# Feed-forward: the product moved to the head of the slot, one pipeline stage fewer, counts shared with VectorE, and the attention's causal mask added on VectorE

## The reference, cut to what matters

```python
def ffn(x, W_syn, b_syn, W_out, b_out, gamma, beta):   # x: 2048 tokens x 512
    z = x @ ternary(W_syn).T + b_syn                   # 2048 x 2048
    thresh = top_k(z, 204)[:, -1:]                     # per row
    hidden = where(z >= thresh, relu(z), 0)
    out = hidden @ ternary(W_out).T + b_out            # 2048 x 512
    return layernorm(x + out, gamma, beta)
x = x + 0.5 * ffn(layernorm(x))
x = x + causal_attention(layernorm(x))                 # 2 sequences of 1024, 16 heads of 32
x = x + 0.5 * ffn(layernorm(x))
```

## Time and profile before

| | |
|---|---|
| median of 3 runs | 1291.21 us (1290.18 to 1293.3) |
| the profiled execution | 1289.8 us |
| its span in the trace | 1288.0 us |
| TensorE busy | 1110.0 us (86%) |
| VectorE busy | 916.6 us (71%) |
| ScalarE busy | 795.9 us (62%) |
| GpSimd busy | 297.3 us (23%) |
| first feed-forward, attention, second feed-forward | about 0 to 384, 384 to 927, 927 to 1288 us |

### The profile page before, as it was taken

The page is one execution under the profiler, slowest core; times in us unless marked ns, Lnnn a source line. Parts: engine busy times, 40 slices in busy tenths (PEclk is TensorE's granted clock), DMA queues, the critical chain, the costliest instruction groups (busy, mean ns, idle before and its releaser), DMA issues.

```text
span 1288.0 us, 17909 instructions
## 1 busy us (share of the span) xinstructions
PE 1110.0 (86%) x6149; PEld 510.9 (40%) x6198; DVE 916.6 (71%) x2010; ACT 795.9 (62%) x1147; POOL 297.3 (23%) x379
## 2 busy tenths in 40 slices
PE   0896999987768789999999799999799799998776
PEld 0342555543334333333344333332244355554333
DVE  5766899889963787875334887782223699999995
ACT  5399888896213536657614356567248998888521
POOL 2100122222252143100220450002100013222224
PEclk9997999998887989999999899999899899999787
DMA  9200000000010122110000311110000000000000
GB/s 370 72 1 1 1 1 2 1 1 1 1 33 21 50 58 50 47 38 2 1 21 8 78 47 46 31 34 2 1 1 1 1 9 10 17 18 18 17 18 33
DMA packets 22284, 37.44 MB, mean 29 GB/s; under 512 B 5398, under 2 KB 7833, under 8 KB 21532
## 3 DMA queue, kind: packets, MB, share of 16 engines
q1 hardware_dynamic: 21404, 34.54, 8.5%
q0 software_dynamic: 768, 1.57, 0.5%
HBM read 19.17 MB, written 4.21 MB: 18 GB/s over the span
## 4 chain that ended last, share of the span: by engine, by line
PE 62%; DVE 20%; issue 7%; ACT 5%; SPq 3%; POOL 1%; DMA 1%; another core or an unknown queue 1%; DVEq 0%; POOLq 0%; ACTq 0%
PE zP L473 13%; PE oP L506 11%; PE xP L619 5%; PE oP L619 5%; PE zP L603 4%; PE zP L544 4%; PE hP L582 3%; PE hP L493 3%; DVE mx L1312 3%; PE hP L644 2%; DVE arena L1095 2%; PE zP L644 2%; DVE arena L1135 2%; ACT arena L738 2%; DVE m L1143 2%
## 5 line engine op out<-in xcount | busy, mean ns | idle before, releaser
L738 ACT ACTIVATE arena<-arena,X 128x2048 int8<-128x2048 f32 x160 | 319.5, 2003 | 4.7 <-DVE X L1127 4.7
L793 ACT ACTIVATE arena<-zP,asc 128x512 f32<-128x512 f32 (+3 forms) x384 | 201.0, 581 | 115.5 <-PE zP L607 84.4
L506 PE MATMUL oP<-T,arena 128*128 128x512 f16 x1024 | 261.2, 402 | 3.0 <-DVE arena L1217 3.0
L473 PE MATMUL zP<-T,arena 128*128 128x512 f16 x1024 | 251.0, 390 | 6.0 <-ACT arena L709 5.1
L1312 DVE TENSOR_REDUCE mx<-hP 128x1 f32<-128x512 f32 (+3 forms) x256 | 135.8, 551 | 36.5 <-PE hP L585 25.0
L719 ACT ACTIVATE arena<-hP,sc 128x512 f16<-128x512 f32 x128 | 88.3, 690 | 106.8 <-PE hP L493 106.8
L473 PEld LDWEIGHTS zP<-T,arena 128*128 128x128 f16 x1024 | 102.3, 100 | 130.3 <-issue 14.6
L506 PEld LDWEIGHTS oP<-T,arena 128*128 128x128 f16 x1024 | 103.4, 102 | 112.1 <-issue 26.3
L709 ACT ACTIVATE arena<-zP,sc 128x512 f32<-128x512 f32 x128 | 87.3, 686 | 81.2 <-PE zP L478 54.8
L603 PE MATMUL zP<-arena 98*128 98x512 f16 (+3 forms) x384 | 110.2, 332 | 2.6 <-DMA arena<-arena 1.7
L1095 DVE SCALAR_TENSOR_TENSOR arena<-hP,sc,arena 128x512 f16<-128x512 f32 x128 | 95.6, 747 | 9.0 <-ACT arena L719 7.9
(11 more groups left out here) (177 smaller groups left out, 1581.6 us busy)
## 6 DMA issues: line engine op xcount, KB each, us to landing
arena<-arena SPq DMA_DIRECT2D x168, 64.0 KB, 2.0
arena<-in_w_synT SPq DMA_DIRECT2D x4, 1024.0 KB, 8.3
arena<-in_w_outT SPq DMA_DIRECT2D x4, 1024.0 KB, 14.7
out_dram<-x_sb SPq DMA_DIRECT2D x16, 256.0 KB, 2.0
x_sb<-in_x SPq DMA_DIRECT2D x3, 1024.0 KB, 14.0
arena<-in_w_o SPq DMA_DIRECT2D x2, 1024.0 KB, 5.0
arena<-arena POOLq DMA_DIRECT2D x24, 64.0 KB, 1.9
arena<-in_b_syn SPq DMA_DIRECT2D x1, 1024.0 KB, 12.1
```

What stands on the lines that cost most here:

```text
L473: pe.matmul(zP[:, c * CW:(c + 1) * CW], part[:, g % 2, k, :], T1[:, k, c * CW:(c + 1) * CW], start=(n == 0 and k == 0), stop=False)
L506: mm = pe.matmul(oP[:, :], part[:, k, :], T2[:, k, :], start=(c == 0 and n == 0 and k == 0), stop=False)
L738: act.activation(junk[:, counted[0] % 2, :], Z[:, g % ZR, :], ACT.Sign, bias=X[:, 2, k:k + 1], accum_out=S[:, k:k + 1]).then_inc(sm["cnt"], 1)
L793: act.activation(PT[:, m // 4 % 2, h, q0:512], colP[m % 3][:, q0:512], ACT.Exp, scale=asc[:, g, 10:11]).then_inc(sm["exp_done"], 1)
```

## The change

The number of the first count's slot becomes a constant, `S_CNT` = 1: count k of tile i now happens in slot i + 1 + k, so that count 0 runs in the slot of the tile's own `mm1`. `S_SEL`, `S_OUT` and `S_FIN` each go down by one (6, 7, 8), and each feed-forward has one slot fewer. The second product is no longer spread over two slots: TensorE's slot becomes `h_turn` c and `mm1` c for c = 0 to 3 (`x_turn` after c = 1), and then `mm2` 0 to 3 with `ok_rows` before chunk 2. ScalarE and VectorE's lists follow that order. Reading the flag and branching on it are taken apart, with `h_lo` 3 between. In slots 3, 4, 5 and 6 one or two of the counts are made on VectorE by `count_here` (`ON_DVE`). In the attention the mask matmul goes away and VectorE adds a bf16 mask tile while it takes the maximum (`tensor_tensor_reduce`, which also writes the sums to `scored`).

```diff
-S_SEL, S_OUT, S_FIN = 2 + NC, 3 + NC, 4 + NC
+S_CNT = 1
+S_SEL, S_OUT, S_FIN = S_CNT + NC, S_CNT + NC + 1, S_CNT + NC + 2
...
-        FIRST_UPD, LAST_UPD = 3, NT + S_SEL - 1
+        FIRST_UPD, LAST_UPD = S_CNT + 1, NT + S_SEL - 1
+        ON_DVE = {S_SEL - 3: (1,), S_SEL - 2: (1, 3), S_SEL - 1: (1, 3), S_SEL: (3,)}
...
                     for c in range(4):
+                        do(h_turn, f, s, S_OUT, c)
                         do(mm1, f, s, 1, c)
+                        if c == 1 and (f, s) != (0, 0):
+                            do(x_turn, f, s, 0)
+                    for c in range(4):
                         if c == 2:
                             do(ok_rows, f, s, S_SEL)
-                        do(h_turn, f, s, S_OUT, c)
-                        if c == 0 and (f, s) != (0, 0):
-                            do(x_turn, f, s, 0)
-                        if c < 2:
-                            do(mm2, f, s, S_OUT + 1, c + 2)
-                        else:
-                            do(mm2, f, s, S_OUT, c - 2)
+                        do(mm2, f, s, S_OUT, c)
...
-                    do(evac, f, s, 2, 3)
-                    do(h_hi, f, s, S_OUT + 1, 3)
+                    do(h_hi, f, s, S_OUT, 0)
                     do(evac, f, s, 1, 0)
-                    do(h_hi, f, s, S_OUT, 0)
+                    count(f, s, 4)
+                    do(h_hi, f, s, S_OUT, 1)
+                    do(evac, f, s, 1, 1)
                     if (f, s) != (0, 0):
                         do(x_hi, f, s, 0)
-                    count(f, s, 4)
                     count(f, s, 3)
-                    do(evac, f, s, 1, 1)
-                    do(h_hi, f, s, S_OUT, 1)
+                    do(h_hi, f, s, S_OUT, 2)
+                    do(evac, f, s, 1, 2)
+                    do(h_hi, f, s, S_OUT, 3)
+                    do(evac, f, s, 1, 3)
                     count(f, s, 2)
                     count(f, s, 1)
-                    do(evac, f, s, 1, 2)
-                    do(h_hi, f, s, S_OUT, 2)
                     count(f, s, 0)
...
+            def count_here(f, s, k):
+                i = at(s, S_CNT + k)
+                if i is None or not on_dve(s, k):
+                    return
+                g = f * NT + i
+                dve.wait_ge(sm["z_evac"], 4 * g + 4)
+                after(0)
+                link(dve.tensor_scalar(hT_mem.bitcast(I8)[:, 0:N], Z[:, g % ZR, :], X[:, 0, k:k + 1], None, ALU.is_gt, ALU.add,
+                                       accum_out=S[:, k:k + 1]))
+                link(dve.tensor_scalar(S[:, k:k + 1], S[:, k:k + 1], 2.0, -float(N), ALU.mult, ALU.add))
...
-                    do(h_lo, f, s, S_OUT + 1, 3)
+                    if s in ON_DVE and s < S_SEL:
+                        for k in range(NC):
+                            count_here(f, s, k)
+                    do(h_lo, f, s, S_OUT, 0)
+                    do(residual, f, s, S_FIN)
                     do(below, f, s, S_SEL)
-                    do(h_lo, f, s, S_OUT, 0)
+                    do(h_lo, f, s, S_OUT, 1)
                     if (f, s) != (0, 0):
                         do(x_lo, f, s, 0)
                     if (f, s) == (0, 1):
                         search_start()
                     do(pick, f, s, S_SEL)
-                    do(h_lo, f, s, S_OUT, 1)
-                    do(residual, f, s, S_FIN)
+                    if s in ON_DVE and s >= S_SEL:
+                        for k in range(NC):
+                            count_here(f, s, k)
+                    do(h_lo, f, s, S_OUT, 2)
                     if (f, s) != (0, -1):
                         do(stats1, f, s, -1)
+                    do(read_flag, f, s, S_SEL)
+                    do(h_lo, f, s, S_OUT, 3)
+                    do(search_if_open, f, s, S_SEL)
                     do(keep_top, f, s, S_SEL)
-                    do(h_lo, f, s, S_OUT, 2)
...
-                        own = c == t // 4
-                        mm = pe.matmul(rowP[bank][:, 0:w], stack[0:3 * HD, 0, h, t * P:(t + 1) * P],
-                                       stack[0:3 * HD, 1, h, 512 * c:512 * c + w], start=True, stop=not own)
-                        if own:
-                            mm = pe.matmul(rowP[bank][:, w - P:w], identm[:, :], maskq[:, :], start=False, stop=True)
...
+                        if c == t // 4:
+                            if m >= 2:
+                                dve.wait_ge(sm["row_max"], m - 1)
+                            dve.tensor_tensor_reduce(scored[:, m % 2, 0:w], rowP[bank][:, 0:w], causal[:, 512 - w:512],
+                                                     1.0, -BIG, ALU.add, ALU.max, mx[:, h, t, c:c + 1])\
+                                .then_inc(sm["row_max"], 1)
```

More of the change, by code:

```diff
@@ L220, in program @@
         identm = sb("identm", [P, P], F16)
-        maskq = sb("maskq", [P, P], F16)
+        causal = sb("causal", [P, 512], BF16)
+        scored = sb("scored", [P, 2, 512], BF16)
         maskk = sb("maskk", [P, P], F16)
@@ L361, in do, with on_dve @@
                 stage(f, i, *a)
-        FIRST_UPD, LAST_UPD = 3, NT + S_SEL - 1
+        FIRST_UPD, LAST_UPD = S_CNT + 1, NT + S_SEL - 1
+        ON_DVE = {S_SEL - 3: (1,), S_SEL - 2: (1, 3), S_SEL - 1: (1, 3), S_SEL: (3,)}
+        def on_dve(s, k):
+            return k in ON_DVE.get(s, ())
         def updates(f, s):
@@ L580, in core @@
                         w = min(512, (t + 1) * P - 512 * c)
-                        own = c == t // 4
-                        mm = pe.matmul(rowP[bank][:, 0:w], stack[0:3 * HD, 0, h, t * P:(t + 1) * P],
-                                       stack[0:3 * HD, 1, h, 512 * c:512 * c + w], start=True, stop=not own)
-                        if own:
-                            mm = pe.matmul(rowP[bank][:, w - P:w], identm[:, :], maskq[:, :], start=False, stop=True)
-                        mm.then_inc(sm["row_ps"], 1)
+                        pe.matmul(rowP[bank][:, 0:w], stack[0:3 * HD, 0, h, t * P:(t + 1) * P],
+                                  stack[0:3 * HD, 1, h, 512 * c:512 * c + w], start=True, stop=True)\
+                            .then_inc(sm["row_ps"], 1)
                     elif kind == "turn":
@@ L724, in count @@
             def count(f, s, k):
-                i = at(s, 2 + k)
-                if i is None:
+                i = at(s, S_CNT + k)
+                if i is None or on_dve(s, k):
                     return
@@ L843, in counts_before, with here @@
         def counts_before(f, s):
-            per_f = NC * NT
-            return f * per_f + sum(1 for t in range(-1, s) for k in range(NC) if at(t, 2 + k) is not None)
+            def here(upto):
+                return sum(1 for t in range(-1, upto) for k in range(NC)
+                           if at(t, S_CNT + k) is not None and not on_dve(t, k))
+            return f * here(NT + S_FIN + 1) + here(s)
         @block.gpsimd
@@ L868, in _ @@
             link(pool.tensor_scalar(identm[:, :], identf[:, :], MASK, None, ALU.mult))
-            link(pool.memset(maskq[:, :], 0.0))
+            link(pool.memset(causal[:, :], 0.0))
             link(pool.memset(maskk[:, :], 0.0))
-            pool.affine_select(out=maskq[:, :], in_=maskq[:, :], compare_op=ALU.is_ge, fill=-MASK, base=0,
-                               pattern=[[-1, P]], channel_multiplier=1).then_inc(sm["masks"], 1)
+            pool.affine_select(out=causal[:, 384:512], in_=causal[:, 384:512], compare_op=ALU.is_ge, fill=-MASK * MASK,
+                               base=0, pattern=[[-1, P]], channel_multiplier=1).then_inc(sm["masks"], 1)
             pool.affine_select(out=maskk[:, :], in_=maskk[:, :], compare_op=ALU.is_ge, fill=-MASK, base=0,
@@ L1201, in search_down, with read_flag @@
                     add_found(HIT, BOUND)
-            def keep_top(f, i):
+            def read_flag(f, i):
                 g = f * NT + i
@@ L1206, in keep_top, with search_if_open @@
                 dve.tensor_copy(oki[:, :], xP[:, 0:1]).then_inc(sm["ok_read"], 1)
+            def search_if_open(f, i):
+                g = f * NT + i
                 dve.wait_ge(sm["ok_read"], g + 1)
@@ L1209, in keep_top @@
                     search_down(Z[:, g % ZR, :])
+            def keep_top(f, i):
+                g = f * NT + i
                 dve.scalar_tensor_tensor(Z[:, g % ZR, :], Z[:, g % ZR, :], TH, Z[:, g % ZR, :], ALU.is_ge, ALU.mult)\
@@ L1248, in normal_rows @@
                     if b == 0:
-                        dve.wait_ge(sm["cnt"], NC * NT)
+                        dve.wait_ge(sm["cnt"], counts_before(1, -1))
                         dve.wait_ge(sm["x_new"], BT)
@@ L1311, in core @@
                         dve.wait_ge(sm["row_ps"], m + 1)
-                        dve.tensor_reduce(mx[:, h, t, c:c + 1], rowP[bank][:, 0:w], AX.X, ALU.max)\
-                            .then_inc(sm["row_max"], 1)
+                        if c == t // 4:
[4 more added lines that the diff above has]
+                                .then_inc(sm["row_max"], 1)
```

(4 more changed lines are left out.)

## The result

The changed kernel takes 1307.1 us (median of 4 runs, 1305.3 to 1308.6), the kernel before in the same comparison 1291.7 us (1290.2 to 1293.3). The ratio is 1.0118, 95% interval 1.0099 to 1.0137: slower by 15.4 us; the prediction said 1306. The profiled execution has a span of 1306.2 us, 18.2 more than before; it is the longest of the four, and the one before was 1.4 us under its median, so the traces show some 3 us more than the medians do.

A forecast was written before the change was run, and what follows sets the result against it. TensorE bounds full slots and the attention's row steps, VectorE the emptying. f=0 +14.4, f=1 +7.8 and attention -7 give +15.2: 1289.8 becomes 1305.0, on the median's scale 1306, range 1296 to 1317 us.

The forecast's parts named there:

- Emptying: Last slots of each block, without mm1: 17.8 us against 15.91 in f=1, 17.5 against 15.6 in f=0.
- the clock stays up: Rival for the emptying: TensorE's chunks and transposes run at full rate, 15.4 us a slot, total 1282; chance 0.11.
- Full slot: Slots with mm1 and mm2: 17.75 us in f=1, 17.45 in f=0, against TensorE's 17.24 before.
- `h_lo` 3 hides wholly behind the branch: Between flag read and keep_top on VectorE: h_lo 3 adds no time; if not hidden, up to 0.66 us more.
- First slot: Slot after the first selection, TensorE idle then restarting slow: 19.8 us in f=1, 19.5 in f=0.
- Filling: Slots up to the first keep_top: VectorE sets f=0, 115.6 against 114.2; f=1 wins 10.2 us; a count costs 2.55.
- K(6): Start of keep_top in slot 6, the first tile's selection: 115.6 us in f=0, 1003.9 in f=1.
- The end: Last tile of each block: all transposes precede mm2, product ends about 15.0 us after keep_top's start, not 17.6: -2.6 us.
- Attention: Row steps: 256 mask matmuls go, 14 us at most; VectorE's maximum costs +0.13 us each; -7 us in all.
- The order costs nothing: Rival: full slots stay at 17.24 us, emptying at 15.6 and 15.9; total 1273, down to 1266; chance 0.25.
- VectorE becomes the attention's bound: Rival for the row steps: maximum +0.33 us and more each, about +25 us per sequence, total 1355; chance 0.05.
- Gains and losses cancel: Rival: count costs its low end (-6 us in f=0), half the slots' losses come, 1288 to 1295; chance 0.12.

The follow-up runs named there:

- Experiment 3: Changed kernel plus 14 unread 512-column matmuls on TensorE ahead of the fourth transpose in each slot of the emptying: 1286.8 us, ratio 0.9971.
- experiment 1: Changed kernel with the flag's row behind the first chunk of mm2 instead of behind the second: 1297.0 us, ratio 1.0044.
- experiment 4: Attention's part alone on the kernel before: 1284.3 us; changed kernel with all counts on ScalarE: 1308.1; that with the stages back one slot: 1327.9.
- experiments 2 and 5: Changed kernel with flag's row ahead of all mm2: 1350.9 us; with h_lo 1 ahead of below: 1299.7, and that with VectorE counts only in f=1: 1302.1.

## Why the prediction was right

*How much of it is luck.* The medians moved by 15.4 us and the prediction said 15.2, but single stretches of the walk above missed by up to 3.4 us, in both directions, and cancel; against the traces the forecast is 3 us short. The kinds of slot cancel too. In f=0 the seven full slots took 123.5 us (122.2 predicted), the two behind them 35.3 (33.8) and the five of the emptying 84.4 (87.5); in f=1 it was 122.5 (124.3), 34.7 (34.4) and 86.8 (89.0). What was right is the mechanism and the sign; the last microseconds were luck.

*Emptying.* The step that decided between forecast and rivals, and shown: in f=1 17.8 us predicted, 17.8 falling to 17.1 measured, against 15.9; in f=0 17.5 predicted and only 16.6 to 17.0 measured, against 15.6. Its cause was the chain of wait, low clock, and flag's row behind two chunks. That the first slot of f=1 fits to 0.03 us is chance: two chunks took 5.71 us to the flag's row where I had 5.27, transpose and flag's row 1.23 where I had 1.36, and the branch 1.03 where I had 1.31. Experiment 3 takes the low clock alone away and gets 15.2 (the rival "the clock stays up" priced it at 15.4 and the total at 1282; made to happen, it gave 1286.8). The slot shrank from 17.8 to 17.1 us because the clock came back earlier within the two chunks: 4.6 us behind their start in the first slot and 3.1 us in the last, so that they took 5.87 us falling to 5.16 (4.62 to 5.08 in f=0). Why it comes back sooner in f=0 the runs don't show. The Trainium skill (TensorE: Matmul & The Clock Gate, What's actually happening) has the clock high only after sustained work; the granted 0.60 behind the wait and 1.00 with the added matmuls agree.

*Full slot.* 17.75 predicted, 17.55 measured in f=1: the 0.3 us for `h_lo` 1 and the flag's place were right (experiment 1: 17.22 when the row moves up). The branch was too dear in f=1, where I carried over its long level (1.31) and it came at the short one (1.03), and too cheap in the later slots of f=0, where I had the short one (1.00) and it took 1.34: those slots took 17.9 where I had 17.45. What switches the level I didn't find. The step "`h_lo` 3 hides wholly behind the branch" held, to 0.03 us.

*First slot.* 19.8 and 19.5 predicted, 20.07 and 19.16 measured.

*Filling.* K(6) in f=0 115.6 predicted, 117.2 measured; the count's 2.55 us was right to 0.03, at the upper bound. The Trainium skill (SBUF — State Buffer, Who interferes with whom) excepts a `tensor_scalar` that also writes out its accumulator from those that can enter the two-port modes; the 2.35 us of this instruction, against 1.28 for a comparison without a sum, agree, though the two also differ in the type of their output (int8 and f16). Kernels with the same filling show 115.3 to 119.0 there, so 1.6 us isn't an error that can be told. In f=1 -10.2 was predicted and -8.4 came; the sign given for it, K(6) near 1004, had left out what f=0 and the attention shift it (it came at 1016.5). What was wrong was my later reading of the parts, in the expectations of experiment 4: I held the stage for worth little and the order for the smaller cost, where they are -19.8 and +43.6. The prediction summed both in one, which is why its total held.

*The end.* -2.6 us twice was predicted, -0.9 and -1.3 came. The last tile's four chunks, TensorE in f=1:

```profile
1288.23 8.43 PE L514 MATMUL oP<-T,arena 128*128 128x512 f16 x32
```

They also start behind a wait, and 8.43 us is 1.2 more than twice the 3.62 of two chunks at the high clock. I had counted the slow return in the slots and forgotten it here.

*Attention.* -7 predicted; -6.3 in the trace, and -7.2 by the medians when changed alone. The sub-step was wrong: VectorE's maximum with the mask added was to cost 0.13 us more each, and it costs nothing (680 ns against 686). TensorE's busy time fell by 11.3 us with the attention's part alone (1110.0 to 1098.7), and 7 came through; in which waits the other 4 went the runs don't show.

*The rivals.* "The order costs nothing", the likeliest of them at 0.25, was 34 us off: the order is the largest single cost of all the parts. "VectorE becomes the attention's bound" fell with the 680 ns of its maximum. "Gains and losses cancel" needed the count at its low end, and it came at the high one; its price was also added up wrongly, since half of the 33 us between 1273 and 1306 and 6 us for the counts give about 1283 by the prediction's own terms, and not 1288 to 1295.

## What to carry to other kernels

Where an engine comes back from a wait at a low clock, ask what is queued behind its first instructions: a small result that stands behind two chunks of product inherits their slowness, and moving it ahead of them only helps as long as the next stage's first instruction doesn't stand behind the rest. An order with long runs of one engine's work and one long wait can lose to an interleaved one with the same work. Unread work in the wait is a cheap test of whether the clock is the cause.

## What the runs showed of the hardware that was not expected

- Fourteen unread matmuls of 512 columns in a wait of 3.97 us raised the granted clock of the slots from 0.80 to 1.00 and took 20 us off the kernel.
- A `tensor_tensor_reduce` with a bf16 mask takes as long as the plain maximum over the same 512 values from PSUM: 680 against 686 ns.
- From the start of the last instruction ahead of the branch to `keep_top` it takes one of two times in most slots, 0.3 us apart, whatever stands further ahead: 1.00 or 1.31 us behind the read alone, 0.85 or 1.16 behind a step of 0.18 us (0.67 or 0.98 idle), 0.96 or 1.26 behind an `h_lo` (0.22 or 0.52 idle). So it reads as if only that last instruction ran beside the branch. (Some slots of experiments 2 and 5 lie between these levels or above them, up to 1.55 behind an `h_lo`.) The level holds for many slots in a row and changes within one block, between the two blocks, and between kernels with the same code there; nothing here shows what sets it. Whoever compares two traces at this place has to compare the same level.
